# A six-layer decoder kernel on one core: the first two weights loaded and split in tiles, the start's loads reordered, the first extra rows issued by two engines

## The chip, the cores and the metric

The kernel runs on one core of a Trainium2 chip. The metric is the device time of one execution in microseconds (us). Engines are named as in the profile: PE (TensorE; PEld is its weight load), DVE (VectorE), ACT (ScalarE), POOL (GpSimd), SP (SyncE, which only issues transfers here); SPq is SP's sequencer.

## The reference, cut to what matters

Two decoder layers over `x` (8 batches, 128 tokens, 512 features, float32). Layer 0: causal attention of 32 heads, autocorrelation against a context, a mixture of 28 low-rank experts. Layer 1: attention with ALiBi slopes, cross attention, routed low-rank heads. A layer norm follows each. The change lies in the first microseconds of layer 0's attention:

```
q = (x @ Wq.T + bq).reshape(b, l, h, hd).transpose(0, 2, 1, 3)
k = (x @ Wk.T + bk).reshape(b, l, h, hd).transpose(0, 2, 1, 3)
v = (x @ Wv.T + bv).reshape(b, l, h, hd).transpose(0, 2, 1, 3)
scores = jnp.einsum('bhqd,bhkd->bhqk', q, k) / math.sqrt(hd)
att = softmax(where(causal, scores, -inf)); out = att @ v;  out @ Wo.T + bo
```

## The kernel before, in words

All of x stays on chip in `x_all`. A float32 product of weights is done in three matmuls (`mm3`, lines 736 to 738) of 128x512, on a high part and a low part of each operand: ACT writes the high part (a cast), DVE the low part (the difference). One product of a batch with a 512x512 weight is four tiles k of three matmuls, 12 in all.

Layer 0's attention is a software pipeline over steps i from -8 on, four steps a batch; each engine runs its own `attention_step(l, i)` in that order, and semaphores tie them. In the start the order of work on PE is: x of batch 0 turned (L791), q of batch 0 (12 matmuls), k of batch 0 (12), x of batch 1 turned, qT of batch 0 turned (L814), kT of batch 0 turned, q and k of batch 1, then step 0: `scores` of step 0 (L855), x of batch 2 turned, qT of batch 1; step 1: `scores` of step 1, v of batch 0, kT of batch 1; step 2: `scores` of step 2, q of batch 2; and so on. Step i's `scores` wait for the row maxima of step i-1, two reductions on DVE (`maxima`, L2045). Three banks of PSUM are shared in turn (`bank_taken`): a product may start when the one two before it has been read.

Weights of layer 0's attention come whole, 1 MB each, by SP. `first_weights(i)` splits one: on ACT two casts of 128x1024 (L1326), on DVE two differences of 128x1024 (L1989). Weights q and k are split before the pipeline starts; v in step -3, o in step 0. On ACT the split of v lies between the two `qk_split` (L1337) of batch 0: that of qT and that of kT. `tables` on DVE (L1993, L1994) makes bf16 copies of the identity and of the mask; it stands before the steps and waits for seven small loads counted on one semaphore, `ld_c`, the last of which is `br_row`. After it come the `biased` additions (L2018) that free q's and k's banks.

The rows of masks and positions that `scores` need beside q and k come by small transfers (`extra_rows`, L661): eight of 16 KB a batch, issued by SP once both of the batch's `qk_split` are done.

SP's order at the start is: x of batch 0, the identity (L632), weight q (L633), bq and bk (L635), small (L636), weight k (L637), the mask (L638), x of batch 1, weight v (L640), bv, bo, br (L641 to L643), weight o (L644), x of batches 2 to 7, two contexts (L622), two pieces of a later weight (L619), and then the extra rows of batch 0.

Of the kernel before, what the change touches and what calls it, by code (L numbers as in the profile page):

```python
# [109 lines left out]
def decoder(nc, a, out):  # L110
# [9 lines left out]
    with es:  # L120
# [178 lines left out]
        ld_w0 = [sem(f"ld_w0_{n}") for n in "qkvo"]  # L299
        ld_masks = sem("ld_masks")  # L300
# [9 lines left out]
        x_loaded = per_slot("x_loaded")  # L310
        x_rest = sem("x_rest")
# [57 lines left out]
        mix_psum = per_slot("mix_psum")  # L369
        mixmax_ready = per_slot("mixmax_ready")  # L370
        mixexp_ready = per_slot("mixexp_ready")
        mixed_ready = per_slot("mixed_ready")
        mixedT_psum = per_slot("mixedT_psum")
        mixedT_ready = per_slot("mixedT_ready")
# [30 lines left out]
        TABLES, EARLY = 2, 7  # L405
# [107 lines left out]
        START = FIRST + 6  # L513

# [19 lines left out]
        def mix(trip, y):  # L534

            return nth(trip, 1, 1, TRIPS if y == FF else 0)
# [71 lines left out]
        def _(sp):  # L608
# [3 lines left out]
            def load_x(b):  # L612
                sp.dma_start(x_all[:, b, :], row(a["x"], b)).then_inc(x_loaded[b] if b < SLOTS else x_rest, 16)
# [41 lines left out]
            def extra_rows(l, b):  # L655

                sp.wait_ge(qk_rows, batch(l, b, 2, 2))
                for e in range(2):
                    for g in range(GROUPS):
                        at = g * PAD + HD * (1 - e) + 1  # L660
                        sp.dma_start(qk[b % RING][at:at + 4, e:e + 3:2, :, :], a["extra"][l, e, g]).then_inc(extra_loaded[b % 2], 16)  # L661

            def self_attention(l):

                pieces, before = ((pieces_during_A0, 0), (pieces_during_A1, PIECES_A1))[l]
                fetch(pieces(0), 0, 2, before, slice(0, 2))
                for i in range(FIRST, LAST):
# [12 lines left out]
                    if of_step(i, "kT") is not None:  # L680
                        extra_rows(l, b + 1)

            for s in both:
                load_context(a["ctx"], s, s)
# [46 lines left out]
        def _(pe):  # L731
# [46 lines left out]
            def x_rows_turned(l, b):  # L778
# [5 lines left out]
                elif b < SLOTS:  # L784
                    pe.wait_ge(x_loaded[b], 16)
                else:
                    pe.wait_ge(x_rest, 16 * (B - SLOTS))
# [6 lines left out]
            def projected(l, kind, b):  # L794
# [85 lines left out]
            def attention_out(l, b):  # L880
# [4 lines left out]
                if l == 0 and b == 0:  # L885
                    pe.wait_ge(w0_ready, 8)
# [126 lines left out]
            def gates_and_rank(trip, s):  # L1013
# [3 lines left out]
                ins.then_inc(mix_psum[s], 1)  # L1017
# [6 lines left out]
            def gated_to_rank(trip, s):  # L1024
                pe.wait_ge(mixed_ready[s], mix(trip, MOE))
# [3 lines left out]
                ins.then_inc(mixedT_psum[s], 1)  # L1029

            def experts_out(trip, s):
                pe.wait_ge(mixedT_ready[s], mix(trip, MOE))
# [101 lines left out]
            def routes_and_low(trip, s):  # L1134
# [5 lines left out]
                ins.then_inc(mix_psum[s], 1)  # L1140

            def low_to_rank(trip, s):
                pe.wait_ge(mixed_ready[s], mix(trip, FF))
                nc.tensor.transpose(bank[s][2][:, 0:P], low[s], ident[:, :]).then_inc(mixedT_psum[s], 1)
# [11 lines left out]
            pe.wait_ge(ld_masks, 16)  # L1156
# [133 lines left out]
        def _(act):  # L1290
# [30 lines left out]

            def first_weights(i):

                act.wait_ge(ld_w0[i], 16)
# [3 lines left out]
            def qk_split(l, i, b):  # L1328
# [5 lines left out]
                if l == 0 and b == RING - 1 and i == 0:  # L1334
                    act.wait_ge(w0_ready, 6)
# [3 lines left out]
                ins.then_inc(qk_rows, 1)  # L1339

# [8 lines left out]
            def probs(l, j):  # L1349
# [3 lines left out]
                if l == 0 and j < STEPS:  # L1353
                    act.wait_ge(w0_ready, 4)
# [12 lines left out]
            def attention_step(l, i):  # L1367
# [15 lines left out]
                if l == 0 and i in (-3, 0):  # L1383
                    first_weights(2 + (i == 0))
# [80 lines left out]
            def gate_exp(trip, s):  # L1465
                act.wait_ge(mixmax_ready[s], mix(trip, MOE))
                av(gates[s][:, 2, 0:NE], gates[s][:, 0, 0:NE], ACT.Exp, bias=st[s][:, ONE_A], scale=1.0
                   ).then_inc(mixexp_ready[s], 1)

            def gated_split(trip, s):  # L1470
                act.wait_ge(mixedT_psum[s], mix(trip, MOE))
# [74 lines left out]
            def route_exp(trip, s):  # L1546
                act.wait_ge(mixmax_ready[s], mix(trip, FF))
                av(st[s][:, EIGHT], st[s][:, EIGHT], ACT.Exp, bias=st[s][:, ONE_A], scale=1.0,
                   accum_out=st[s][:, ONE_B]).then_inc(mixexp_ready[s], 1)

            def low_copied(trip, s):
                act.wait_ge(mixedT_psum[s], mix(trip, FF))
# [12 lines left out]
            for i in range(2):  # L1565
                first_weights(i)
# [917 lines left out]
```

## Time and profile before

| | us |
|---|---|
| median of 3 runs (lowest to highest) | 955.42 (952.87 to 955.94) |
| the profiled execution | 953.89 |
| its span | 952.1 |
| PE busy in the span | 873.2 (92%) |
| first weight matmul of q | 12.44 |
| first `scores` matmul | 34.53 |

Times in the rows are us from the span's start. The span is what the profiler's rows cover; the execution's time holds 1.8 us around it. A timeline row gives start, duration, engine, line, operation and tiles, and, in brackets, how long the engine had been idle and who released it. A chain row gives start, length and what stood on the chain that ended last. A windows row gives the busy time of each engine in a stretch, then PE's granted clock (1.00 is full), the share of time that the DMA engines were busy, and GB/s.

### The profile page before, as it was taken

To read this page: it belongs to the slowest core of one execution; us is meant where nothing else is said; L and a number is where in the kernel's file an instruction comes from. 1 tells how busy PE (TensorE), PEld (TensorE's weight loads), DVE (VectorE), ACT (ScalarE), POOL (GpSimd) and SP (SyncE) were. 2 spreads that over 40 slices of the span, in tenths; PEclk is the share of its full clock that TensorE was granted. 3 is DMA by queue.
4 is the path that set the end of the run, shared out by engine and by line. 5 is a ranking of instruction groups with operands and counts; after the bars stand their busy time and mean duration, and the time that the engine had idled before them with its cause. 6 is when DMAs were issued, how large, how long until landed. Compare 5 with 4: busy or idle time off the path is not lost.

```text
span 952.1 us, 21348 instructions
## 1 busy us (share of the span) xinstructions
PE 873.2 (92%) x8680; PEld 697.4 (73%) x8680; DVE 584.5 (61%) x1506; ACT 395.5 (42%) x976; POOL 340.9 (36%) x356
## 2 busy tenths in 40 slices
PE   4899999797798989889999898999999999999995
PEld 3677777564444767667777677888998898889983
DVE  3445565657796556546666553797376747765765
ACT  3334444343555233224343333553454364526532
POOL 1111223267877346544777355770000000010001
PEclk9799999998999999889999899999999999999997
DMA  8100000122232110000000011231000010000001
GB/s 315 43 19 26 19 14 19 42 80 78 85 96 60 67 44 19 5 19 19 18 18 24 17 28 55 87 103 36 23 2 1 1 45 1 2 1 23 2 2 44
DMA packets 20945, 38.09 MB, mean 40 GB/s; under 512 B 3232, under 2 KB 7456, under 8 KB 20336
## 3 DMA queue, kind: packets, MB, share of 16 engines
q1 hardware_dynamic: 20848, 36.73, 12.4%
q8 instruction: 69, 1.13, 0.5%
q14 instruction: 28, 0.23, 0.1%
HBM read 30.20 MB, written 2.10 MB: 34 GB/s over the span
## 4 chain that ended last, share of the span: by engine, by line
PE 71%; DVE 11%; POOL 6%; issue 4%; DMA 3%; ACT 2%; SPq 2%; POOLq 0%; DVEq 0%; ACTq 0%
PE bank L736 15%; PE bank L737 14%; PE bank L738 14%; PE bank L855 7%; PE bank L1119 6%; PE bank L876 3%; DVE tank L2255 2%; PE bank L829 2%; PE bank L814 2%; DVE tank L2265 2%; PE bank L860 1%; DMA br_row<-br_dram 1%; PE bank L755 1%; DVE tank L2045 1%; PE bank L1150 1%
## 5 line engine op out<-in xcount | busy, mean ns | idle before, releaser
L736 PE MATMUL bank<-wr,hTl 128*128 128x512 f32 (+3 forms) x472 | 191.9, 407 | 10.8 <-DVE wr L1989 7.6
L737 PE MATMUL bank<-wr,hTh 128*128 128x512 f32 (+3 forms) x472 | 182.4, 386 | 0.0
L738 PE MATMUL bank<-wr,hTh 128*128 128x512 f32 (+3 forms) x472 | 182.2, 386 | 0.0
L2045 DVE TENSOR_REDUCE tank<-bank 128x4 f32<-128x512 f32 x128 | 82.4, 686 | 70.7 <-PE bank L829 70.7
L736 PEld LDWEIGHTS bank<-wr,hTl 128*128 128x128 f32 (+1 forms) x472 | 91.2, 193 | 35.6 <-issue 16.9
L1358 ACT ACTIVATE pT<-bank 128x512 f32<-128x512 f32 x128 | 69.5, 595 | 96.9 <-PE bank L829 96.8
L738 PEld LDWEIGHTS bank<-wr,hTh 128*128 128x128 f32 (+1 forms) x472 | 90.5, 192 | 17.8
L737 PEld LDWEIGHTS bank<-wr,hTh 128*128 128x128 f32 (+1 forms) x472 | 91.1, 193 | 15.4 <-issue 1.2
L855 PE MATMUL bank<-qk 32*128 32x128 f32 x1024 | 79.7, 297 | 15.3 <-DVE tank L2045 5.8
L855 PEld LDWEIGHTS bank<-qk 32*128 32x128 f32 x1024 | 66.9, 198 | 31.6 <-issue 24.6
L1337 ACT ACTIVATE qk<-bank,small_sb 128x512 f32<-128x512 f32 x64 | 46.3, 774 | 75.6 <-PE bank L814 75.6
L860 PE MATMUL bank<-qk 32*128 32x128 f32 x1024 | 77.0, 290 | 0.3 <-DMA qk<-tank 0.3
L736 PE MATMUL bank<-hTh,wr 128*128 128x256 f32 (+1 forms) x240 | 73.3, 305 | 1.5 <-DVE hTl L2226 1.5
L737 PE MATMUL bank<-hTl,wr 128*128 128x256 f32 (+1 forms) x240 | 73.0, 304 | 0.0
L738 PE MATMUL bank<-hTh,wr 128*128 128x256 f32 (+1 forms) x240 | 72.9, 304 | 0.0
L1775 POOL TENSOR_TENSOR stats<-stats,half 128x1 f32<-128x1 f32 x8 | 4.4, 548 | 180.2 <-DVE stats L2300 180.2
L1536 ACT ACTIVATE tank<-bank,stats 128x256 f32<-128x256 f32 x128 | 58.6, 482 | 21.7 <-DVE stats L2249 21.7
L860 PEld LDWEIGHTS bank<-qk 32*128 32x128 f32 x1024 | 64.5, 192 | 4.0 <-issue 3.0
L1119 PE MATMUL bank<-tank 128*32 128x128 f32 (+1 forms) x1024 | 53.8, 284 | 2.8 <-DVE tank L2255 1.8
L1764 POOL TENSOR_TENSOR stats<-stats,half 128x1 f32<-128x1 f32 x16 | 9.9, 621 | 127.0 <-DVE stats L2134 126.8
L2248 DVE TENSOR_REDUCE stats<-bank 128x2 f32<-128x512 f32 x64 | 43.7, 684 | 17.6 <-PE bank L738 17.6
L2255 DVE COPY tank<-bank 128x512 f32<-128x512 f32 x64 | 39.7, 682 | 21.8 <-PE bank L1108 21.8
(234 smaller groups left out, 1898.4 us busy)
## 6 DMA issues: line engine op xcount, KB each, us to landing
raw<-w_qkv_dram SPq DMA_DIRECT2D x12, 256.0 KB, 3.1
raw<-w_xq_dram SPq DMA_DIRECT2D x16, 192.0 KB, 2.3
raw<-w_xo_dram SPq DMA_DIRECT2D x12, 256.0 KB, 2.7
x_all<-x_dram SPq DMA_DIRECT2D x8, 256.0 KB, 11.5
cin<-ctx_dram SPq DMA_DIRECT2D x8, 256.0 KB, 3.2
qk<-extra_dram SPq DMA_DIRECT2D x128, 16.0 KB
cin<-ctxT_dram SPq DMA_DIRECT2D x8, 256.0 KB, 2.9
out_dram<-x_all SPq DMA_DIRECT2D x8, 256.0 KB, 2.0
```

The source lines that it names most:

```text
L736: mm(dst, lhs[1], rhs[0], start=start, stop=False)
L737: mm(dst, lhs[0], rhs[1], start=False, stop=False)
L738: return mm(dst, lhs[0], rhs[0], start=False, stop=stop)
L855: ins = mm(s_bank[n][:, at], qk[b % RING][g, e, m, :], qk[b % RING][g, 2 + e, m, :], start=m == 0, stop=True, skip_group_check=True)
L860: ins = mm(t_bank[n][:, at], qk[c % RING][g, 2 + f, m, :], qk[c % RING][g, f, m, :], start=m == 0, stop=True, skip_group_check=True)
L1119: ins = mm(bank[s][0][row:row + n, tile * P:(tile + 1) * P], xv[s][:, t * NKV + g * XD + first:t * NKV + g * XD + first + n], xpT[s][:, (2 ...
L1337: ins = av(qk[b % RING][:, 2 * i + e, :, :], tiles(m_bank[u % 2][:, :]), ACT.Identity, bias=row_shift[:, 2 * i + e:2 * i + e + 1], scale=r ...
L1358: av(pT[e][:, 2 * rows + n, :], t_bank[n][:, :], ACT.Exp).then_inc(exp_ready, 1)
L1536: ins = av(xp[s][:, h * XT:(h + 1) * XT], bank[s][i][:, j * XT:(j + 1) * XT], ACT.Exp, bias=st[s][:, NEGMAX.start + h:NEGMAX.start + h + 1 ...
L2045: v.tensor_reduce(nm[b % 2][:, at:at + KT], s_bank[n][:, :].rearrange("p (m t) -> p m t", m=KT), AX, ALU.max, negate=True).then_inc(max_re ...
L2248: steps_done(XA, trip, v.tensor_reduce(r, bank[s][i][:, :].rearrange("p (h t) -> p h t", h=2), AX, ALU.max))
L2255: v.tensor_copy(xpT[s][:, i * 512:(i + 1) * 512], bank[s][i][:, :]).then_inc(xpT_ready[s], 1)
```

## The change

The loads of weights q and k are cut in four tiles of 128x512 each, with a semaphore each, and so are their splits; PE waits tile by tile. The order of SP's loads is changed: bq follows q's tiles and bk follows k's; x of batch 2 comes right behind bv; weight o, x of batches 3 to 7, the contexts and the pieces of the later weight are issued after the extra rows of batch 0. The small loads that `tables` waits for are four now (bq, bk, small, mask); bv, bo and br are counted on another semaphore, for which DVE's `values` of batch 0 and POOL's first `add_bias` wait. Weights v and o are split in steps -1 and 4, on DVE after that step's `biased`. Of the eight extra rows of batch 0 ACT issues four. To free semaphores, six pairs (one semaphore per slot) are merged to one each, with counts that go over both slots.

```diff
-        ld_w0 = [sem(f"ld_w0_{n}") for n in "qkvo"]
-        ld_masks = sem("ld_masks")
+        ld_w0_tiles = [[sem(f"ld_w0_{n}{k}") for k in range(KT)] for n in "qk"]
+        ld_w0 = [sem(f"ld_w0_{n}") for n in "vo"]
-        mix_psum = per_slot("mix_psum")
+        mix_psum = sem("mix_psum")
...
-        TABLES, EARLY = 2, 7
+        TABLES, EARLY, ROWS = 2, 4, 3
+        W0_TILES = 2 * KT
+        W0_STEPS = (-1, 4)
...
-        def mix(trip, y):
-            return nth(trip, 1, 1, TRIPS if y == FF else 0)
+        def mix(trip, s, y):
+            return row_of(trip + (TRIPS if y == FF else 0), s)
...
             load_x(0)
-            sp.dma_start(ident[:, :], a["masks"][:, 0:P]).then_inc(ld_masks, 16)
-            sp.dma_start(raw_w0(0), a["w0_q"]).then_inc(ld_w0[0], 16)
-            for i, n in enumerate(("bq", "bk")):
-                sp.dma_start(by_column[i], a[n].partition_broadcast(P)).then_inc(ld_c, 16)
+            sp.dma_start(ident[:, :], a["masks"][:, 0:P]).then_inc(x_loaded[0], 16)
+            for i, n in enumerate("qk"):
+                for k in range(KT):
+                    at = slice(k * D, (k + 1) * D)
+                    sp.dma_start(raw_w0(i)[:, at], a["w0_" + n][:, at]).then_inc(ld_w0_tiles[i][k], 16)
+                sp.dma_start(by_column[i], a["b" + n].partition_broadcast(P)).then_inc(ld_c, 16)
             sp.dma_start(small[:, :], a["small"]).then_inc(ld_c, 16)
-            sp.dma_start(raw_w0(1), a["w0_k"]).then_inc(ld_w0[1], 16)
             sp.dma_start(causal, a["masks"][:, P:]).then_inc(ld_c, 16)
             load_x(1)
-            sp.dma_start(raw_w0(2), a["w0_v"]).then_inc(ld_w0[2], 16)
-            sp.dma_start(bv_row, a["bv"].partition_broadcast(P)).then_inc(ld_c, 16)
-            sp.dma_start(bo_row, a["bo"].partition_broadcast(P)).then_inc(ld_c, 16)
-            sp.dma_start(br_row[:, :], a["br"].partition_broadcast(P)).then_inc(ld_c, 16)
-            sp.dma_start(raw_w0(3), a["w0_o"]).then_inc(ld_w0[3], 16)
-            for b in range(SLOTS, B):
-                load_x(b)
+            sp.dma_start(raw_w0(2), a["w0_v"]).then_inc(ld_w0[0], 16)
+            sp.dma_start(bv_row, a["bv"].partition_broadcast(P)).then_inc(ld_rows, 16)
+            load_x(2)
+            sp.dma_start(bo_row, a["bo"].partition_broadcast(P)).then_inc(ld_rows, 16)
+            sp.dma_start(br_row[:, :], a["br"].partition_broadcast(P)).then_inc(ld_rows, 16)
...
                 for e in range(2):
-                    for g in range(GROUPS):
-                        at = g * PAD + HD * (1 - e) + 1
-                        sp.dma_start(qk[b % RING][at:at + 4, e:e + 3:2, :, :], a["extra"][l, e, g]).then_inc(extra_loaded[b % 2], 16)
+                    if (l, b, e) != (0, 0, 0):
+                        for g in range(GROUPS):
+                            at = g * PAD + HD * (1 - e) + 1
+                            sp.dma_start(qk[b % RING][at:at + 4, e:e + 3:2, :, :], a["extra"][l, e, g]).then_inc(extra_loaded[b % 2], 16)
...
                     if of_step(i, "kT") is not None:
                         extra_rows(l, b + 1)
+                    if l == 0 and of_step(i, "kT") == 0:
+                        fetch(pieces(0), 0, 2, before, slice(0, 2))
+                        sp.dma_start(raw_w0(3), a["w0_o"]).then_inc(ld_w0[1], 16)
+                        for n in range(RING, B):
+                            load_x(n)
+                        for s in both:
+                            load_context(a["ctx"], s, s)
...
 PE, projected:
-                if l == 0 and b == 0:
-                    pe.wait_ge(w0_ready, 2 * (i + 1))
                 for k in range(KT):
+                    if l == 0 and b == 0:
+                        pe.wait_ge(w0_ready, KT * i + k + 1 if kind in "qk" else W0_TILES + 2)
...
 ACT:
+            def first_tiles(i):
+                for k in range(KT):
+                    act.wait_ge(ld_w0_tiles[i][k], 16)
+                    copy(w_qkv0[i][0][:, k], tiles(raw_w0(i))[:, k]).then_inc(w0_hi, 1)
+            def extra_rows_of_first():
+                act.wait_ge(qk_rows, 2)
+                for g in range(GROUPS):
+                    at = g * PAD + HD + 1
+                    act.dma_start(qk[0][at:at + 4, 0:3:2, :, :], a["extra"][0, 0, g]).then_inc(extra_loaded[0], 16)
                 if of_step(i - 1, "kT") is not None:
                     qk_split(l, 1, b + 1)
+                    if l == 0 and b + 1 == 0:
+                        extra_rows_of_first()
...
-                if l == 0 and i in (-3, 0):
-                    first_weights(2 + (i == 0))
+                if l == 0 and i in W0_STEPS:
+                    first_weights(2 + W0_STEPS.index(i))
...
 POOL, ahead of the steps:
-            pool.wait_ge(ld_c, 16 * EARLY)
+            pool.wait_ge(ld_rows, 16 * ROWS)
 DVE (values of batch 0 waits for ld_rows too):
+            def first_tiles(i):
+                for k in range(KT):
+                    dve.wait_ge(w0_hi, KT * i + k + 1)
+                    v.tensor_tensor(w_qkv0[i][1][:, k], tiles(raw_w0(i))[:, k], f32(w_qkv0[i][0][:, k]), ALU.subtract).then_inc(w0_ready, 1)
-                if l == 0 and i in (-3, 0):
-                    first_weights(2 + (i == 0))
                 for n, kind in enumerate("qk"):
                     if of_step(i, kind) is not None:
                         (biased, clipped)[l](n, b + 2)
+                if l == 0 and i in W0_STEPS:
+                    first_weights(2 + W0_STEPS.index(i))
             for i in range(2):
-                first_weights(i)
-            dve.wait_ge(ld_masks, 16)
+                first_tiles(i)
+            dve.wait_ge(x_loaded[0], 32)
             dve.wait_ge(ld_c, 16 * EARLY)
             tables()
```

## Rows read from the trace of the kernel before

**Rows 1.** The page, busy time of the engines

```profile
PE 873.2 (92%) x8680; PEld 697.4 (73%) x8680; DVE 584.5 (61%) x1506; ACT 395.5 (42%) x976; POOL 340.9 (36%) x356
```

**Rows 2.** The chain of waits, 0 to 80 us: start, length, what

```profile
8.40 10.69 DMA br_row<-br_dram
19.19 1.36 DVE ident L1993
...
30.50 4.03 issue
34.53 1.96 PE bank L855 x16
...
46.28 1.09 PE bank L855 x16
...
62.66 0.31 PE bank L855 x2
```

**Rows 3.** Timeline, 0 to 21 us: start, duration, engine, line, operation

```profile
4.88 0.58 ACT L1320 CAST hTh<-bank 128x512 fp32r<-128x512 f32 x1 [2.88 <-PE bank L791]
5.50 0.69 DVE L1983 TENSOR_TENSOR hTl<-bank,hTh 128x512 fp32r<-128x512 f32 x1 [5.50 <-ACT hTh L1320]
8.86 1.99 ACT L1326 CAST wr<-pT 128x1024 fp32r<-128x1024 f32 x2 [3.40 <-DMA pT<-w_q_dram]
9.94 2.36 DVE L1989 TENSOR_TENSOR wr<-pT,wr 128x1024 fp32r<-128x1024 f32 x2 [3.75 <-ACT wr L1326]
12.44 0.77 PE L736 MATMUL bank<-wr,hTl 128*128 128x512 f32 x1 [7.60 <-DVE wr L1989]
17.68 0.40 PE L736 MATMUL bank<-wr,hTl 128*128 128x512 f32 x1
20.25 0.40 PE L738 MATMUL bank<-wr,hTh 128*128 128x512 f32 x1
20.57 1.27 DVE L2018 TENSOR_TENSOR tank<-bank,tank 128x512 f32<-128x512 f32 x2
```

**Rows 4.** Timeline, 21 to 26 us

```profile
21.99 0.63 PE L814 MATMUL bank<-ident,tank 128*128 128x128 f32 x4
22.66 1.45 ACT L1337 ACTIVATE qk<-bank,small_sb 128x512 f32<-128x512 f32 x2
23.52 0.63 PE L814 MATMUL bank<-ident,tank 128*128 128x128 f32 x4 [0.90 <-DVE hTl L1983]
24.00 2.00 ACT L1326 CAST wr<-qk 128x1024 fp32r<-128x1024 f32 x2
```

**Rows 5.** Transfers, 0 to 60 us: KB, issue to landing; line L661, 26 to 36, then 0 to 60

```profile
pT<-w_k_dram SPq DMA_DIRECT2D x1, 1024.0 KB, 9.8
...
L661 SPq DMA_DIRECT2D qk<-extra_dram x8: 613/628/834, 27.4 to 32.2; - x8
...
L661 SPq DMA_DIRECT2D qk<-extra_dram x16: 613/627/834, 27.4 to 52.4; - x16
```

**Rows 6.** The loads of x (line L613), 0 to 60 us: issue to landing

```profile
DMA to landing us min/median/max: 2.8/11.5/12.0
```

**Rows 7.** Windows of 1 or 2 us

```profile
5.00:6.00 1.00, 0.00 (x0) 0.00 (x0) 0.50 (x1) 0.47 (x1) 0.00 (x0) 1.00 0.76 262
6.00:7.00 1.00, 0.00 (x0) 0.00 (x0) 0.19 (x1) 0.00 (x0) 0.00 (x0) 1.00 0.97 389
22.00:23.00 1.00, 0.62 (x5) 0.38 (x4) 0.32 (x1) 0.93 (x2) 0.89 (x1) 1.00 1.07 406
35.00:36.00 1.00, 1.00 (x12) 1.00 (x12) 0.00 (x0) 0.00 (x0) 0.00 (x0) 0.50 0.00 0
```

**Rows 8.** Timeline, 44 to 60 us

```profile
44.98 0.40 PE L736 MATMUL bank<-wr,hTl 128*128 128x512 f32 x1
57.41 1.45 ACT L1337 ACTIVATE qk<-bank,small_sb 128x512 f32<-128x512 f32 x2
59.17 1.29 DVE L2045 TENSOR_REDUCE tank<-bank 128x4 f32<-128x512 f32 x2 [0.93 <-PE bank L829]
```

More of the change, by code:

```diff
@@ L310, in decoder @@
         x_loaded = per_slot("x_loaded")
+        x_third = sem("x_third")
         x_rest = sem("x_rest")
@@ L368, in decoder @@
         mixture_ready = sem("mixture_ready")
-        mix_psum = per_slot("mix_psum")
[L370 to L374, printed above, removed]
+        mix_psum = sem("mix_psum")
+        mixmax_ready = sem("mixmax_ready")
+        mixexp_ready = sem("mixexp_ready")
+        mixed_ready = sem("mixed_ready")
+        mixedT_psum = sem("mixedT_psum")
+        mixedT_ready = sem("mixedT_ready")
         inner_hi = per_slot("inner_hi")
@@ L612, in load_x @@
             def load_x(b):
-                sp.dma_start(x_all[:, b, :], row(a["x"], b)).then_inc(x_loaded[b] if b < SLOTS else x_rest, 16)
+                sp.dma_start(x_all[:, b, :], row(a["x"], b)).then_inc((*x_loaded, x_third)[b] if b < RING else x_rest, 16)
             def fetch(pieces, trip, per_trip, before, which):
@@ L658, in extra_rows @@
                 for e in range(2):
-                    for g in range(GROUPS):
-                        at = g * PAD + HD * (1 - e) + 1
-                        sp.dma_start(qk[b % RING][at:at + 4, e:e + 3:2, :, :], a["extra"][l, e, g]).then_inc(extra_loaded[b % 2], 16)
+                    if (l, b, e) != (0, 0, 0):
+                        for g in range(GROUPS):
+                            at = g * PAD + HD * (1 - e) + 1
+                            sp.dma_start(qk[b % RING][at:at + 4, e:e + 3:2, :, :], a["extra"][l, e, g]).then_inc(extra_loaded[b % 2], 16)
             def self_attention(l):
                 pieces, before = ((pieces_during_A0, 0), (pieces_during_A1, PIECES_A1))[l]
-                fetch(pieces(0), 0, 2, before, slice(0, 2))
+                if l == 1:
+                    fetch(pieces(0), 0, 2, before, slice(0, 2))
                 for i in range(FIRST, LAST):
@@ L681, in self_attention @@
                         extra_rows(l, b + 1)
-            for s in both:
-                load_context(a["ctx"], s, s)
+                    if l == 0 and of_step(i, "kT") == 0:
+                        fetch(pieces(0), 0, 2, before, slice(0, 2))
+                        sp.dma_start(raw_w0(3), a["w0_o"]).then_inc(ld_w0[1], 16)
[3 more added lines that the diff above has]
+                            load_context(a["ctx"], s, s)
             self_attention(0)
@@ L784, in x_rows_turned @@
                 elif b < SLOTS:
-                    pe.wait_ge(x_loaded[b], 16)
+                    pe.wait_ge(x_loaded[b], 32 if b == 0 else 16)
+                elif b < RING:
+                    pe.wait_ge(x_third, 16)
                 else:
-                    pe.wait_ge(x_rest, 16 * (B - SLOTS))
+                    pe.wait_ge(x_rest, 16 * (B - RING))
                 u = m_uses[l, "x", b]
@@ L1139, in routes_and_low @@
                     ins = mm(bank[s][2][:, 0:NL], plain_hT[:, k, s, 1, :], w_al[:, k, :], start=k == 0, stop=k == KT - 1)
-                ins.then_inc(mix_psum[s], 1)
+                ins.then_inc(mix_psum, 1)
             def low_to_rank(trip, s):
-                pe.wait_ge(mixed_ready[s], mix(trip, FF))
-                nc.tensor.transpose(bank[s][2][:, 0:P], low[s], ident[:, :]).then_inc(mixedT_psum[s], 1)
+                pe.wait_ge(mixed_ready, mix(trip, s, FF))
+                nc.tensor.transpose(bank[s][2][:, 0:P], low[s], ident[:, :]).then_inc(mixedT_psum, 1)
             def heads_out(trip, s):
@@ L1353, in probs @@
                 if l == 0 and j < STEPS:
-                    act.wait_ge(w0_ready, 4)
+                    act.wait_ge(w0_ready, W0_TILES)
                 if b > 0 or l == 1:
@@ L2000, in values @@
                 dve.wait_ge(consts_ready, ONES[l])
+                if l == 0 and b == 0:
+                    dve.wait_ge(ld_rows, 16 * ROWS)
                 if b >= 2:
```

51 lines of the change are left out of this document (25 added, 26 removed).

## The prediction

> **What bounds the kernel now.** The page comes first: PE is busy 92% of the span [rows 1], so what can go is a stretch in which PE waits or runs slowly. The windows of the start show one, 0 to 46 us. Second, the chain of waits over that stretch: it runs through SP's issues to `br_row`'s landing at 19.1, DVE's `tables`, then PE, and has a hole of 4.03 us ahead of the first `scores` [rows 2]. Third, the timelines, which show what PE lacked in each gap: the split of q [rows 3], the two `qk_split` with the split of v between them [rows 4]. Last, the transfers [rows 5, 6]. From `scores` of step 2 (46.28) PE is nearly always busy up to 100 us, and everything behind is tied to the pipeline's steps, not to the clock on the wall; so I take the time at which `scores` of step 2 start as the measure, and look for what is given back behind it.
>
> **The parts.** All times are those of the profiled execution.
>
> 1. Tiles of q. Weight q landed at 8.86 and its first product began at 12.44, behind two casts and two differences [rows 3]. In the change the same bytes precede the last tile, so it lands at 8.86 again; the bytes behind tile 0 are three tiles, 0.79 MB, which at 262 to 389 GB/s [rows 7] take 2.0 to 3.0 us. I take 2.5: tile 0 lands at 6.3, the others some 0.85 apart. A tile's split costs 0.6 on ACT (0.58 for a cast of 128x512) and 0.69 on DVE, with 0.1 between [rows 3]: ready at 7.7. Floor: DVE is busy with x until 6.19, so 6.9. Ceiling: the tiles land together at 8.86, ready at 10.2. A tile feeds 3 matmuls at half clock, 1.3 us (12 took 12.44 to 17.68 [rows 3]), slower than tiles arrive, so PE doesn't wait again. q runs 7.7 to 12.95, k at the full pitch (17.68 to 20.65, 2.97 us) 12.95 to 15.9. Weight k landed at 13.6 (3.78 + 9.8 [rows 5]); its last tile, now ahead of bk and small, is no later, is ready by 15.0, and its 0.7 us of matmuls fit. k ends 4.75 us earlier.
>
> 2. `tables` no longer wait for `br_row`. The first `biased` ended at 21.2, the second at 21.84, and qT began at 21.99, 1.34 behind k's end. Now `biased` of q can be done during k: qT begins 0.85 behind k's end, at 16.75, 5.2 us earlier. The L1993 copy took 1.36 us for 128 columns [rows 2]. If it takes that again right behind the last split, `biased` of q ends at 17.2 and qT is 1.2 us later. I take none of it, since in the change POOL's first addition waits for bv, bo and br.
>
> 3. Split of v. From qT's start to the end of kT's `qk_split`, at which the first extra row is issued, there are 5.35 us (21.99 to 27.36) [rows 4, 5], of which ACT's two casts of v hold 1.9 [rows 4]. Without them kT's rows are ready at 20.2, 7.1 us earlier. The cover is kT's turning, which ends 2.2 us behind qT's start.
>
> 4. Extra rows. Eight issues, 0.63 us each and 0.69 apart, with the landing made 7.17 us (27.36 to 34.53) [rows 2, 5]. Four on each engine save four pitches, 2.8 us: landed at 24.6. At the same time q and k of batch 1 (12 matmuls each, k free to start when kT's rows are ready) end at 24.7. So both ends meet, and `scores` of step 0 begin at 24.75, 9.8 us earlier. Lower bound of the saving here: the transfers of the two engines go one behind the other, as eight in one queue do, and nothing of the 2.8 comes. On ACT the issues stand ahead of the split of v, which then runs 23.0 to 25.0.
>
> 5. A new wait. DVE's half of v's split now stands behind `biased` of k (24.7 to 25.4) and takes 2.36 us: 25.4 to 27.75. The maxima of step 0 queue behind it, 27.75 to 29.05. PE has `scores` of step 0 (1.4 at full clock, chain row 46.28 with its mask), x and qT turned until 27.4, then waits for those maxima, 1.7 us. Steps 1's `scores`, v (2.9) and kT (0.6) follow: `scores` of step 2 at 34.1.
>
> 6. Clock. Behind the hole of 4.03 us PE's granted clock was 0.50 [rows 7], the lower of its two levels, 1.2 GHz, and matmuls had the long pitch until 44.98 [rows 8]. `scores` of step 0 to those of step 2 took 11.75 us; mine take 9.35 with the new wait in. The saving at `scores` of step 2 is 46.28 - 34.1 = 12.2.
>
> 7. Split of o in step 4. ACT would do it behind the `qk_split` that ends at 58.86, DVE 3.35 us later has its lower part (24.00 to 27.35 for v [rows 4]), at 62.2. Maxima of step 5 began at 59.17 [rows 8] and would now end at 63.5, where PE wants them at 62.66 [rows 2]: 0.9 us lost. The bounds are 0 and 2.4, its whole time on DVE.
>
> 8. At nothing: the merged semaphores (each engine goes through slot 0, then slot 1, as before), the loads moved behind the extra rows (3.3 MB at 406 GB/s [rows 7], 8 us from 23 on, landed near 33; x of batch 3 is wanted at step 4, near 44, the piece that ACT splits in step 1 lands first), POOL's additions. The extra rows of batch 1 are the cover that could go. Their last issue stood at 52.4 [rows 5]; with the 2.3 us from last issue to first use in batch 0 (32.2 to 34.53) they landed near 54.7, and `scores` of step 4 began near 55 (two steps of 4.3 us behind 46.28): no slack. In the change they may be issued from 35.6 on. SP's ten moved issues, from 23 on at 0.5 to 0.9 us, end at 28 to 32, and their bytes have landed near 33, so I count nothing; if they took longer than to 35.6, each further us would be lost.
>
> Sum: 12.2 - 0.9 = 11.3 us. The profiled execution gives 953.89 - 11.3 = 942.6; the median of the runs is 1.5 above it, so I predict 944.1.
>
> Two rules of the Trainium skill bear on this. The first, in "DMA: Bandwidth & Descriptors", section Bandwidth, says to batch transfers to 1 MiB or more to get three quarters of the peak. Weight q's loads go against it, but loads of 256 KB with rows of 2 KB ran at 406 GB/s when queued behind each other [rows 7]; by that rule the last tile of k would be late, as in the rival on the other side. The second, same page, section Issuing engines are not separate DMA queues, says that issuing on several engines saves only the sequencer's own time, usually small. Here the eight issues are most of the hole, so by the trace the saving of part 4 stands and by the rule's word "small" it would shrink to the case of one behind the other.
>
> **The rivals.**
>
> Tiles don't come early. The 16 engines' shares of the tiles finish together, and PE starts at 10.2. For: the long landing times of queued loads (9.8 and 11.5 us) [rows 5, 6] show that many are in flight. Against: they land in order. Price 2.5: 946.6.
>
> The clock stays low. Between 24.75 and 29.1 PE does little; if the clock falls there, v and the `scores` run at the long pitch, as at 35 to 45 us. For: the fall behind a wait of 4 us. Against: from 20.65 to 24.2 PE was idle nearly half the time and kept its pitch. Price: v 2.2, `scores` 1.0, the rest 0.3: 3.5, so 947.6.
>
> The extra rows of two engines go one behind the other. Then they land at 27.4; the maxima end at 30.1 instead of 29.05, since v's split is already done, so the wait of part 5 takes most of it. Price 1.3 at most: 945.4. This is also the case in which the change doesn't do what it says.
>
> The other side, slower. Each tile costs what a lone load costs, 2.8 us issue to landing (the shortest of x's [rows 6]). Nine loads (eight tiles, bq) from 3.7 on end at 29; k's product ends at 31 instead of 20.65, 10.4 later, of which parts 2 to 7 give back 6.5: 959. It decides from 2.4 us a tile on (k's end at 27.2). A queued pace of 0.7 (256 KB at 389 to 406 GB/s [rows 7]) speaks against it. In a milder form, near 2.4, there is no change; so there is if a later stage gives the whole saving back, for which I see no transfer or engine tied to absolute time.
>
> **How the numbers follow.** My case 0.58; tiles late 0.12; clock 0.13; one behind the other 0.07; no change 0.06; slower 0.04. The time is my case's, 944.1. Its own bounds are the floor of part 1 (-0.8), part 7 at 0 (-0.9) and, above, `tables` (+1.2) and part 7 whole (+1.5), to which the spread of the runs before adds 2.5 below and 0.5 above. The range goes from 938.5, which also leaves room for the wait of part 5 not coming (-1.7), to 950, where the tiles' and the clock's prices meet. About 0.3% (2.9 us) is what a measurement of this kernel can tell from no change: faster by more 0.90, within 0.06, slower 0.04.
>
> **What would show it.** In the changed kernel's timeline: the first L736 matmul at 7.7 (right within 1); k's last matmul near 15.9; the first L855 near 24.75, against 34.53; a wait of 1 to 2 us of PE for L2045 ahead of the second group of L855; the third group near 34; no granted clock of 0.50 between 20 and 45 us; a wait of near 1 us for L2045 in step 6. The forecast fails if PE's first weight matmul comes after 10, or if the interval from `scores` of step 2 to the end, 905.8 us now (952.1 - 46.3), grows by more than 3 us.

## The result, and the profile after

The changed kernel takes 943.24 us (median of four runs; 940.63 to 944.06) where the kernel before, run beside it, takes 954.9: a ratio of 0.9882, 95% interval 0.9861 to 0.9904, 11.7 us less. Its profiled execution took 944.06, 9.8 less than the one before. The forecast was 944.1.

The page of the changed kernel, busy time of the engines, answers to [rows 1]. Neither PE's work nor its share has changed to speak of; the span has.

```profile
span 942.2 us, 21361 instructions
PE 870.5 (92%) x8680; PEld 695.7 (74%) x8680; DVE 582.5 (62%) x1510; ACT 396.8 (42%) x980; POOL 340.8 (36%) x356
```

The timeline of the changed kernel's start, the marks that the prediction named (start, duration, engine, line, operation; rows between them are left out; lines 745, 802, 825, 866, 2078 are 736, 791, 814, 855, 2045 of before):

```profile
5.61 0.62 ACT L1336 CAST wr<-pT 128x512 fp32r<-128x512 f32 x1 [0.20 <-DMA pT<-w_q_dram]
7.10 0.77 PE L745 MATMUL bank<-wr,hTl 128*128 128x512 f32 x1 [2.31 <-DVE wr L2014]
...
13.89 0.22 DVE L2024 CAST ident<-ident 128x128 bf16<-128x128 f32 x1
14.13 0.68 DVE L2051 TENSOR_TENSOR tank<-bank,tank 128x512 f32<-128x512 f32 x1
15.36 0.60 PE L802 MATMUL bank<-ident,x_all 128*128 128x128 f32 x4
16.39 0.63 PE L825 MATMUL bank<-ident,tank 128*128 128x128 f32 x4 [0.44 <-DVE tank L2051]
...
23.18 1.99 ACT L1342 CAST wr<-qk 128x1024 fp32r<-128x1024 f32 x2 [3.33 <-issue]
24.96 1.16 PE L866 MATMUL bank<-qk 32*128 32x128 f32 x16 [0.48 <-issue]
25.13 2.35 DVE L2020 TENSOR_TENSOR wr<-qk,wr 128x1024 fp32r<-128x1024 f32 x2
27.40 1.28 DVE L2078 TENSOR_REDUCE tank<-bank 128x4 f32<-128x512 f32 x2
28.73 1.16 PE L866 MATMUL bank<-qk 32*128 32x128 f32 x16 [1.36 <-DVE tank L2078]
30.15 0.80 PE L745 MATMUL bank<-wr,hTl 128*128 128x512 f32 x1
34.97 1.16 PE L866 MATMUL bank<-qk 32*128 32x128 f32 x16
```

To be seen: PE starts on the first tile, 5.3 us ahead of [rows 3]; the first `scores` come at 24.96 instead of 34.53, with 0.48 us of pause where 4.03 were [rows 2]; ahead of the second, at 28.73, stands the new wait of 1.36 us for the maxima, which had queued behind v's split; and the third, at 34.97, is 11.2 us ahead of the same matmul before (46.21 in that kernel's timeline; its chain, [rows 2], has the step's `scores` from 46.28).

Windows of the changed kernel between the second and third `scores`; PE's granted clock is the number behind POOL's. It fell to 0.50 (1.2 GHz, the lower level) for 3.4 us, where before it was 0.50 for 10.2 us from 34.7 on [rows 7, 8]:

```profile
29.00:30.00 1.00, 1.00 (x24) 0.83 (x22) 0.28 (x1) 0.19 (x1) 0.72 (x1) 0.92 0.96 391
30.00:31.00 1.00, 1.00 (x10) 0.75 (x3) 0.73 (x2) 0.00 (x0) 0.00 (x0) 0.50 1.05 399
31.00:32.00 1.00, 1.00 (x3) 0.74 (x3) 0.56 (x1) 0.00 (x0) 0.00 (x0) 0.50 1.05 391
32.00:33.00 1.00, 1.00 (x4) 0.78 (x3) 0.00 (x0) 0.00 (x0) 0.00 (x0) 0.50 1.04 399
33.00:34.00 1.00, 1.00 (x6) 0.79 (x5) 0.00 (x0) 0.00 (x0) 0.00 (x0) 0.88 1.03 385
```

And the timeline of step 4 to 6, where o is split now; it answers to [rows 8]:

```profile
47.50 2.00 ACT L1342 CAST wr<-tank 128x1024 fp32r<-128x1024 f32 x2
48.59 2.36 DVE L2020 TENSOR_TENSOR wr<-tank,wr 128x1024 fp32r<-128x1024 f32 x2 [1.59 <-ACT wr L1342]
50.86 1.28 DVE L2078 TENSOR_REDUCE tank<-bank 128x4 f32<-128x512 f32 x2
52.20 0.38 PE L866 MATMUL bank<-qk 32*128 32x128 f32 x2 [0.78 <-DVE tank L2078]
```

The lead of the changed kernel, matching matmul for matmul (both have 8680): 5.3 at the first product, 6.0 at the turning of x of batch 1, 9.6 at the first `scores`, 9.9 at the second, 11.2 at the third, 10.4 from step 6 on, 8.9 from 171 us on, 8.3 from 332, 8.5 from 640, 9.9 at the last. So in this pair of traces the start gives 10.4, and the code behind it, which is the same, moves it by 2.1 down and 1.5 up: a fall of the clock at 163 us lasts 6.8 us where before it lasted 3.4, and the last one begins 7.8 us ahead of the end where before it did 12.9. A second trace of each kernel (experiment 9) gives 8.5 at the third `scores`, 7.6 from step 6 on and 9.8 at the last: what the start gives is 7.6 to 10.4 us, by the execution.

### The profile page after: what moved, and what is told of

Its sections match the earlier page's. It is cut to its first block, busy times and chain, and to the rows that moved or that the text cites. A ratio compares the mean times of both kernels' runs of the same rounds, so it can differ in the third digit from the quotient of the medians.

```text
span 942.2 us, 21361 instructions
## 1 busy us (share of the span) xinstructions
PE 870.5 (92%) x8680; PEld 695.7 (74%) x8680; DVE 582.5 (62%) x1510; ACT 396.8 (42%) x980; POOL 340.8 (36%) x356
## 4 chain that ended last, share of the span: by engine, by line
PE 73%; DVE 10%; POOL 6%; issue 4%; DMA 3%; ACT 2%; SPq 2%; POOLq 0%; DVEq 0%; ACTq 0%
PE bank L745 16%; PE bank L746 15%; PE bank L747 15%; PE bank L866 6%; PE bank L1130 6%; PE bank L887 3%; DVE tank L2288 2%; PE bank L840 2%; PE bank L825 1%; PE bank L871 1%; DVE tank L2298 1%; DVE tank L2078 1%; PE bank L764 1%; SPq L664 1%; PE bank L1150 1%
## 5 line engine op out<-in xcount | busy, mean ns | idle before, releaser
L746 PEld LDWEIGHTS bank<-wr,hTh 128*128 128x128 f32 (+1 forms) x472 | 91.3, 194 | 15.4 <-issue 1.2
L1353 ACT ACTIVATE qk<-bank,small_sb 128x512 f32<-128x512 f32 x64 | 46.2, 775 | 76.4 <-PE bank L825 76.4
L1569 ACT CAST hTh<-bank 128x384 fp32r<-128x384 f32 x32 | 15.3, 480 | 91.0 <-PE bank L1130 91.0
```

Source lines behind the costliest of these rows:

```text
L746: mm(dst, lhs[0], rhs[1], start=False, stop=False)
L1353: ins = av(qk[b % RING][:, 2 * i + e, :, :], tiles(m_bank[u % 2][:, :]), ACT.Identity, bias=row_shift[:, 2 * i + e:2 * i + e + 1], scale=r ...
```

## The experiments

Each is one kernel, profiled once and timed beside the kernel before on one chip (955.3 beside experiments 1 to 4, 953.7 beside 5 to 8, 953.6 beside the second runs of experiment 8 and those of 9). Times of one kernel scatter by 5 to 10 us, so the medians carry the size of an effect and the marks of the start its cause. In experiments 1 to 3 the 95% intervals of the ratio overlap that of the changed kernel (0.9861 to 0.9904): their 2 us in the median are not clear of the scatter, and only the marks speak there. The marks scatter too: the second trace of the kernel before has them 1.4 to 2.0 us earlier, with weight q landed at 7.45 and not at 8.86. "First", "second" and "third" are the starts of the `scores` of steps 0, 1 and 2; lines shift by a few between the kernels.

| kernel | median us | first product | x of batch 1 turned | first | second | third |
|---|---|---|---|---|---|---|
| before | 954.9 | 12.4 | 21.4 | 34.5 | 38.7 | 46.2 |
| before, second trace | 952.9 | 11.0 | 20.0 | 33.2 | 36.7 | 44.8 |
| changed | 943.2 | 7.1 | 15.4 | 25.0 | 28.7 | 35.0 |
| changed, second trace | 943.1 | 6.9 | 15.2 | 24.8 | 28.6 | 36.4 |
| whole loads | 945.7 | 9.8 | 18.2 | 28.2 | 31.6 | 36.3 |
| extra rows by SP | 945.4 | 7.1 | 15.1 | 26.8 | 29.6 | 34.3 |
| v split early | 945.2 | 7.0 | 15.1 | 26.6 | 29.4 | 34.1 |
| `tables` behind br | 951.8 | 6.9 | 21.4 | 32.0 | 35.9 | 42.2 |
| loads in front | 947.6 | 7.1 | 15.6 | 29.4 | 33.6 | 41.8 |
| before, 4 extra rows by ACT | 948.0 | 11.8 | 21.4 | 32.4 | 35.2 | 41.0 |
| tiles alone | 953.6 | 7.4 | 21.9 | 35.7 | 40.0 | 47.1 |
| low parts on POOL | 939.5 | 7.5 | 15.1 | 24.5 | 27.3 | 32.0 |
| low parts on POOL, second trace | 940.6 | 7.6 | 15.3 | 25.0 | 27.8 | 32.5 |

**1. Whole loads.**

```diff
-                for k in range(KT):
-                    sp.dma_start(raw_w0(i)[:, at], a["w0_" + n][:, at]).then_inc(ld_w0_tiles[i][k], 16)
+                sp.dma_start(raw_w0(i), a["w0_" + n]).then_inc(ld_w0_tiles[i][0], 16)
...
-                    act.wait_ge(ld_w0_tiles[i][k], 16)
+                    act.wait_ge(ld_w0_tiles[i][0], 16)
```

> The changed kernel, with weights q and k loaded whole again (one transfer each, in the same place of SP's order); split and waited for in tiles as in the changed kernel. Theory (the tiles' early landing starts PE): all four tiles land when the whole did before, 8.9, the first product begins at 8.9 + 0.6 + 0.7 + 0.15 = 10.3 instead of 7.1, and the third group of `scores` comes near 38 instead of 35.0; near 946.3, 3 us over the changed kernel's 943.2. Rival 1 (loads of 256 KB cost bandwidth, so whole loads land earlier as a sum): PE starts later, but k's last tile lands well before 12, and the loss is under 1 us. Rival 2 (the gain of the start came from the split in tiles on ACT and DVE, not from the loads): the first product begins before 9.

945.67 (942.31 to 947.65), ratio to before 0.9897 (0.9858 to 0.9936). Its timeline where the weights arrive:

```profile
8.33 2.18 ACT L1334 CAST wr<-pT 128x512 fp32r<-128x512 f32 x4 [3.08 <-DMA pT<-w_q_dram]
9.82 0.76 PE L743 MATMUL bank<-wr,hTl 128*128 128x512 f32 x1 [5.18 <-DVE wr L2012]
12.29 2.18 ACT L1334 CAST wr<-pT 128x512 fp32r<-128x512 f32 x4 [1.78 <-DMA pT<-w_k_dram]
```

The first product came at 9.8, and the 2.7 us ran through to the second `scores` (+2.9); the third is only 1.4 later than in the changed kernel's trace, since no fall of the clock came in this one. The early landing of tile 0 (5.61 against 8.33) is these 2.7 us of the start, so rival 2 is out. But the split in tiles has a share of its own: from landing to first product it takes 1.49 us here and in the changed kernel, 3.58 in the kernel before (8.86 to 12.44 [rows 3]). Of the 5.3 us by which PE starts earlier, 2.1 come from the split. Rival 1 is out too: weight k, whole, was there at 12.29, hardly before the last tile's cast of the changed kernel (12.6), and the first two `scores` kept the whole delay.

**2. Extra rows by SP.**

```diff
-                    if (l, b, e) != (0, 0, 0):
-                        for g in range(GROUPS):
+                    for g in range(GROUPS):
...
-                    if l == 0 and b + 1 == 0:
-                        extra_rows_of_first()
```

> The changed kernel, with all eight extra rows of batch 0 issued by SP again. Theory (the issuing sequencer is the price, 0.63 to 0.69 us each): the first `scores` begin 7.2 us after the first issue, near 27.0 instead of 24.97, since eight issues end 2.8 us later; the maxima of step 0 then no longer wait for v's split, so the second group of `scores` comes near 30.0 instead of 28.7, and the pause of PE from 24.5 to 27 may lengthen the fall of the clock from 3.4 to 6.8 us or more. 945 to 947, against 943.2. Rival (two engines' transfers go one behind the other anyway): the first `scores` stay at 25.0 and the time at 943.2.

945.41 (942.15 to 949.92), 0.9896 (0.9866 to 0.9927). Its timeline:

```profile
24.90 2.35 DVE L2017 TENSOR_TENSOR wr<-qk,wr 128x1024 fp32r<-128x1024 f32 x2
26.80 1.16 PE L865 MATMUL bank<-qk 32*128 32x128 f32 x16 [2.54 <-issue]
28.23 1.29 DVE L2075 TENSOR_REDUCE tank<-bank 128x4 f32<-128x512 f32 x2 [0.98 <-PE bank L839]
29.58 1.16 PE L865 MATMUL bank<-qk 32*128 32x128 f32 x16 [0.37 <-DVE tank L2075]
```

The first `scores` are 1.8 us later, the second 0.9: half of the delay is cover for v's split. At the first `scores` the issues are the price, as the theory has it. Over the whole, nothing is lost in this trace: its third `scores` come 0.7 earlier than the changed kernel's, which had a fall of the clock there, and it took 942.15. The longer fall of the clock that I had thought possible is not there: behind a pause of 2.54 us there was none at all.

**3. v split early.**

```diff
-        W0_STEPS = (-1, 4)
+        W0_STEPS = (-3, 4)
```

> The changed kernel, with v split in step -3 again, between the two `qk_split` of batch 0 on ACT (o stays in step 4). Theory: kT's rows come 1.9 us later, so the extra rows are issued near 21.8 and the first `scores` begin near 26.9 instead of 24.97; but DVE is then free for the maxima, PE no longer waits 1.36 us for them, and the second group comes near 29.7 instead of 28.7: 1 us lost, 944.2 (with the fall of the clock unchanged). Rival (the wait for the maxima is what lets the clock fall): no granted clock of 0.50 between 25 and 40 us, and 942 to 943. Second rival (the moved split is worth its whole 1.9 us): 945.1.

945.23 (942.34 to 950.85), 0.9908 (0.9882 to 0.9935). First 26.6, second 29.4, as the theory said. No granted clock of 0.50 between 25 and 40 us, which is the first rival's sign; its time isn't there, for the median is 2 us over the changed kernel's, though this is within the scatter, and the profiled execution (942.34) would have fitted.

**4. `tables` behind br.**

```diff
             dve.wait_ge(ld_c, 16 * EARLY)
+            dve.wait_ge(ld_rows, 16 * ROWS)
             tables()
```

> The changed kernel, with `tables` on DVE waiting for bv, bo and br as before. Theory (the tiles' gain hangs on this edit: `biased` of q queues behind `tables`, and br lands at 18.95): `tables` start near 19.0 and end near 20.4 (POOL adds at the same time), x of batch 1 is turned from 21.1 on instead of 15.4, the first `scores` come near 30.5, and the time is near 949, 5 to 6 us over the changed kernel's. Rival (as the prediction sized this edit, 0.5 us): 943.7.

951.76 (947.86 to 954.01), 0.9973 (0.9949 to 0.9997). Its timeline between k's end and the next matmul:

```profile
19.18 1.26 POOL L1733 TENSOR_TENSOR x_all<-x_all,tank 128x512 f32<-128x512 f32 x1 [17.02 <-DMA br_row<-br_dram]
19.23 1.29 DVE L2024 CAST ident<-ident 128x128 bf16<-128x128 f32 x1 [5.24 <-DMA br_row<-br_dram]
20.44 0.18 DVE L2025 CAST causal<-tank 128x64 bf16<-128x64 f32 x1
20.55 1.27 DVE L2051 TENSOR_TENSOR tank<-bank,tank 128x512 f32<-128x512 f32 x2
21.37 1.09 PE L802 MATMUL bank<-ident,x_all 128*128 128x128 f32 x4 [6.25 <-DVE tank L2051]
```

One wait on three small loads, the last of 4 KB, costs 6.0 us at this mark, and 8.5 in the median: behind PE's pause of 6.25 us the clock fell at 20.1 for 6.8 us as well, which the expectation of 949 had left out. In the kernel before, the same wait cost almost nothing, because k ended at the same time as `tables`.

**5. The kernel before with four of the extra rows by ACT.**

```diff
+                    if (l, b, e) != (0, 0, 0):
...
...
+                    if l == 0 and b + 1 == 0:
+                        extra_rows_of_first()
```

> The kernel before with one edit: ACT issues four of the eight extra rows of batch 0. Theory (each of the change's effects is there by itself, and the pause of 4.03 us is what let the clock fall for 10.2 us): the first `scores` begin 2.8 us earlier, near 31.8; PE's pause shrinks to 1.3 us, the clock keeps its upper level, and `scores` of step 2 come near 39.5 instead of 46.3: near 948. Rival 1 (the clock falls there whatever the pause, since the stretch of small matmuls behind it is weak work): 2.8 us gained only, 952. Rival 2 (no gain without the tiles): 954.9.

948.02 (946.74 to 952.05), 0.9947 (0.9928 to 0.9966) of 953.73. Its timeline:

```profile
32.43 1.16 PE L856 MATMUL bank<-qk 32*128 32x128 f32 x16 [1.90 <-issue]
35.21 1.16 PE L856 MATMUL bank<-qk 32*128 32x128 f32 x16 [0.38 <-DVE tank L2055]
37.33 2.36 DVE L1999 TENSOR_TENSOR wr<-tank,wr 128x1024 fp32r<-128x1024 f32 x2 [1.58 <-ACT wr L1327]
39.61 1.28 DVE L2055 TENSOR_REDUCE tank<-bank 128x4 f32<-128x512 f32 x2
40.95 1.16 PE L856 MATMUL bank<-qk 32*128 32x128 f32 x16 [0.93 <-DVE tank L2055]
```

A pause of 1.90 us instead of 4.03, and no fall of the clock: the first `scores` are 2.1 us earlier, the third 5.3 (0.8 and 3.9 against the second trace of the kernel before, whose start was early throughout, with the same pause of 4.02). This one edit brings half of the change's gain. It also uncovers a wait: o's split in step 0, hidden before by v's product at the long pitch, now delays the maxima, and PE waits 0.93 us for them (with the first `scores` 0.6 us later than expected, the 1.5 by which the third mark missed 39.5).

**6. Tiles alone.** Weights q and k in tiles (loads, splits, waits), everything else as before. The diff is against the changed kernel; SP's order of loads, DVE's order in steps -3 and 0 and the issuer of the extra rows are set back too.

```diff
-        W0_STEPS = (-1, 4)
+        W0_STEPS = (-3, 0)
...
             dve.wait_ge(ld_c, 16 * EARLY)
+            dve.wait_ge(ld_rows, 16 * ROWS)
             tables()
```

> Tiles alone: weights q and k are loaded and split in tiles and waited for by tile, while the order of all loads, `tables` behind br, the steps of v's and o's splits, DVE's order and the eight extra rows by SP are those of the kernel before. Theory (the tiles' 5.3 us are taken back at once by `tables`, which wait for br at 19.1): the first product begins near 7.1, k ends near 16, and from the turning of x of batch 1 on (21.4) everything is where it was: 953 to 955, no gain. Rival (the tiles carry the gain): 949.

953.61 (948.09 to 957.62), 0.9995 (0.9971 to 1.002). The waits of this kernel from 10 to 25 us (engine, line, what it waited for: us in total, times, longest):

```profile
PEld bank L801 <- issue: 5.4, 1, 5.4
PE bank L801 <- DVE tank L2048: 5.0, 1, 5.0
DVE ident L2021 <- DMA br_row<-br_dram: 3.9, 1, 3.9
```

All 5 us of the early start wait for br. The clock fell at 21.4, behind this pause, for 6.8 us, and at 35.0 for 10.2, with a pause of 3.18 us ahead of the first `scores`. The part that gives the change its name gains nothing alone.

**7. Loads in front.**

```diff
+                if l == 0:
+                    sp.dma_start(raw_w0(3), a["w0_o"]).then_inc(ld_w0[1], 16)
+                    for n in range(RING, B):
+                        load_x(n)
+                    for s in both:
+                        load_context(a["ctx"], s, s)
+                fetch(pieces(0), 0, 2, before, slice(0, 2))
...
```

> The changed kernel, with weight o, x of batches 3 to 7, the two contexts and the two pieces of a later weight issued ahead of the extra rows of batch 0, as before. Theory (the extra rows queue behind 3.3 MB): the bulk lands near 27.5, so the extra rows, issued at 19.9, land behind it near 28.5 or later, instead of 24.9; the second group of `scores` comes near 31.5, the clock falls for longer, and the time is 946 to 949. Rival (small transfers pass the bulk, or SP's issue order doesn't matter): first `scores` at 25, 943.2.

947.64 (945.44 to 950.5), 0.9942 (0.9923 to 0.9961). The same eight extra rows, issued at the same time by the same two engines:

```profile
19.83 2.87 SPq L664 DMA_DIRECT2D qk<-extra_dram x4
19.84 3.24 ACTq L1360 DMA_DIRECT2D qk<-extra_dram x4
...
29.38 2.08 PE L864 MATMUL bank<-qk 32*128 32x128 f32 x16 [5.14 <-issue]
```

All eight were there only at 29.4, 4.4 us later, and with the pause of 5.14 us came a fall of 13.7 us. ACT's own queue helps little past SP's bulk: the packets of its four transfers moved between 24.1 and 27.4, where in the changed kernel they moved between 21.4 and 24.4, so they ended 3.0 us later; SP's own four, behind the bulk in the same queue, came last. The third `scores` are 6.8 later and the median 4.4. From there to the last matmul this trace took 894.5 us where the changed kernel's took 899.9, and had the clock low for 44 us in all where that had it low for 58; so the one doesn't measure the other to the microsecond.

**8. Low parts on POOL.** POOL computes the low part of v's second half in step -1 and of o in step 4; DVE keeps v's first half and waits for o's before its tank is written again.

```diff
-                for e in range(2):
+                for e in range(1 if i == 2 else 0):
...
+                if l == 0 and i == W0_STEPS[0]:
+                    pool.wait_ge(w0_hi, W0_TILES + 2)
+                    nc.gpsimd.tensor_tensor(half_w0(2, 1, 1), raw_half(2, 1), f32(half_w0(2, 0, 1)), ALU.subtract).then_inc(w0_ready, 1)
...
```

> The changed kernel, with the low part of v's second half and both halves of o's low part computed on POOL instead of DVE. Theory (DVE's queue is what makes PE wait ahead of the second `scores`, 1.36 us, and in step 6, 0.8 us): the maxima of step 0 begin near 26.4, the second group of `scores` near 27.8 instead of 28.7, the wait in step 6 is gone, and with a shorter pause the clock may stay up (another 1.7 us): 939.8 to 941.5. Rival (POOL's difference of 128x1024 takes over 3 us, or slows DVE beside it, and v's product waits for it instead): the second group is earlier but v's first matmul is at 30 or later, as now, and only step 6's 0.8 us are gained: 942.4.

> The kernel with the low parts of v's second half and of o on POOL once more, on one chip with the changed kernel. Theory (PE's two waits for DVE are gone, 1.4 and 0.8 us, as its first trace showed, and at times 1.7 us of low clock): 2 to 4 us under the changed kernel in the same call, near 939. Rival (its 939.5 was the scatter between chips and executions): within 1 us of the changed kernel.

939.52 (936.26 to 943.69), 0.9861 (0.9829 to 0.9894), and a second time, on one chip with the changed kernel, 940.64 (936.79 to 946.99), 0.9859 (0.9823 to 0.9894). The first trace:

```profile
24.64 1.22 DVE L2027 TENSOR_TENSOR wr<-qk,wr 128x1024 fp32r<-128x1024 f32 x1
24.74 3.32 POOL L1783 TENSOR_TENSOR wr<-qk,wr 128x1024 fp32r<-128x1024 f32 x1 [3.10 <-ACT wr L1342]
25.93 1.29 DVE L2085 TENSOR_REDUCE tank<-bank 128x4 f32<-128x512 f32 x2
27.28 1.16 PE L866 MATMUL bank<-qk 32*128 32x128 f32 x16 [0.37 <-DVE tank L2085]
28.59 0.50 PE L745 MATMUL bank<-wr,hTl 128*128 128x512 f32 x1
```

Both waits for DVE are gone (0.37 us remain of 1.36, and step 6 follows the third `scores` by 16.4 us instead of 17.2), and neither trace had the clock fall before 160 us. POOL's difference did take over 3 us, as the rival has it, but it was done at 28.06, ahead of v's first matmul. The medians are 3.7 and 2.5 us below those of the changed kernel; the ranges overlap, and so do the intervals of the ratio on the one chip (0.9823 to 0.9894 against 0.9842 to 0.9904). All twelve times, with a median of 939.8, stand against ten with 943.1. At step 6 the two traces lead the changed kernel's two by 3.8 and 4.7 us, of which 1.5 and 3.1 are that kernel's fall of the clock; 2.3 and 1.7 are left for the two waits and the start's scatter.

**9. The changed kernel and the kernel before once more.**

> The changed kernel once more, unedited, for a second trace of its start and more times on one chip with the two others of this call. Theory (the fall of the clock at 30 us in its first trace came by chance of time, since two variants with pauses of 2 to 2.5 us before their `scores` had none): the same marks, first product near 7.1, first `scores` near 25.0, second near 28.7, and either a fall of 3.4 us again or none; with none, `scores` of step 2 near 33.3 instead of 35.0. 941 to 944. Rival (the 1.36 us wait for the maxima brings the fall each time): 0.50 between 29 and 34 us again, `scores` of step 2 at 35.0.

> The kernel before once more, for a second trace of its start. Theory (a pause of 4.03 us lets the clock fall in every execution, while how long it stays low varies): a granted clock of 0.50 from about 34 on for 6.8 or 10.2 us, `scores` of step 0 at 34.5 and of step 2 near 46.3 or 44.5; 954. Rival (this fall too comes by chance): no 0.50 before 100 us, `scores` of step 2 near 42.

943.09 (939.01 to 945.24), ratio 0.9873 (0.9842 to 0.9904); and 952.87 (948.21 to 955.19) for the kernel before. The changed kernel's second trace has the clock fall again, earlier and for 6.8 us; windows of 4 us (PE's granted clock again behind POOL's number):

```profile
24.00:28.00 4.00, 2.71 (x34) 1.97 (x32) 3.65 (x5) 2.20 (x5) 1.18 (x1) 1.00 0.86 215
28.00:32.00 4.00, 3.44 (x27) 2.83 (x28) 2.15 (x4) 1.00 (x3) 1.14 (x2) 0.58 0.99 382
32.00:36.00 4.00, 4.00 (x13) 3.09 (x12) 0.24 (x1) 0.00 (x0) 0.00 (x0) 0.56 0.61 228
```

Its third `scores` came at 36.4. The second trace of the kernel before has a fall of 10.2 us too, at 34.0, behind a pause of 4.02; its first product came at 11.0 instead of 12.4, so the lead at that mark is 3.9 to 5.6 us, by the pair of executions that one takes. The fall in both traces of the changed kernel and none in experiments 1, 2, 3, 5 and 8 fit the rival of the expectation better than mine, and experiment 4 fits it too: a wait of 1.55 us for the maxima, and a fall of 3.4 us at 37.1. But experiments 2 and 3 had longer pauses, ahead of the first `scores`, without a fall, and no run took away that wait and nothing else; so the wait goes with the fall in three traces of three and is not shown to be its cause.

## Why the prediction was right, step by step

The time (944.1 against 943.24) and the sign were right, by the mechanism of my case, with part of a rival in it. That the two lie within 0.9 us is luck in part: the profiled execution was forecast at 942.6 and took 944.06, 1.5 too slow, and the median, put 1.5 above the profiled execution, came 0.8 below it; the two errors cancelled.

Part 1, right and a little small. Tile 0 landed at 5.6, not 6.3, as its split began then; PE started at 7.10 (forecast 7.7) and k ended at 15.4 (15.9). The forecast 4.7 us at this mark were 2.6 of landing and 2.2 of the finer split; measured were 3.3 and 2.1. The ceiling of 10.2 was near what whole loads give (9.8, experiment 1).

Part 2, right at the mark (qT at 16.39, forecast 16.75), but mis-weighed. I sized the edit by what it changes beside the other edits, half a microsecond. Taken away alone it costs 6.0 us at the turning of x and 8.5 in all (experiment 4), and without it part 1 is worth nothing (experiment 6). The L1993 copy took 0.22 us, so the bound of 1.36 did not come.

Part 3, right: kT's rows were ready at 19.87 (forecast 20.2). Alone it is worth 1.6 at the first `scores` and 0.6 at the second (experiment 3), since it brings part 5's wait with it.

Part 4, right: the first `scores` at 24.96 (24.75), and the lower bound of transfers one behind the other is refuted for a free queue by experiment 2. It holds where there is bulk ahead (experiment 7).

Part 5, right: a wait of 1.36 us (1.7), the second `scores` at 28.73 (29.1).

Part 6 failed in its step on the clock, though not in the time of the whole. The sum had the clock up from 24.75 on; in both traces of the changed kernel it fell, for 3.4 and 6.8 us. In the first the third `scores` came 34.97 - 28.73 = 6.2 us behind the second, where the traces without a fall have 4.7: 1.5 us (3.1 in the second trace), against the 3.5 that the rival priced. The second mark had come 0.4 earlier than forecast and the stretch without a fall is 0.3 shorter (4.73 against 5.0), which leaves the 0.9 between the forecast 34.1 and 34.97. Why the clock fell there stays open (experiment 9).

Part 7, right: 0.78 us of wait (0.9), and experiment 8 takes it away.

Part 8: nothing late showed. The extra rows of batch 1 were issued from 36.55 on, behind SP's last moved issue at 28.8, and PE had no wait ahead of `scores` of step 4. Experiment 7 shows what moving the loads buys: 4.4 us.

The sum of 11.3 is 9.8 in both pairs of traces and 11.7 in the medians (10.5 in the second timing of the changed kernel, 943.09 beside 953.63). What the trace lacks is 0.9 at the third mark and 0.6 from the later stages (the interval from there to the end, 905.8 before, is 907.2), within the 3 us that I had allowed. The range's lower end is 0.3 above what its own terms give (944.1 - 0.8 - 0.9 - 1.7 - 2.5 = 938.2), which changes nothing here.

Of the rivals: tiles landing together is out (experiment 1 against the trace); the one on the other side, a lone load's cost for each tile, too: the casts of q's four tiles ran from 5.61 to 9.04, at most 1.4 us apart. The rule of the Trainium skill ("DMA: Bandwidth & Descriptors", Bandwidth) on large transfers is about the rate, and the rate may well have dropped a little: from 4 to 12 us the DMA engines moved 300 GB/s with the cut loads and 334 with the whole ones, in one trace each. That did not make k's last tile late enough to matter, and the first tile started PE 2.7 us earlier. What the same page says under Issuing engines are not separate DMA queues agrees in one half, that transfers of all issuers run on the same DMA engines (experiment 7), and the sequencer's time, which it calls usually small beside the DMA itself, was 1.8 us at the first `scores` (experiment 2).

## What to carry to other kernels

At a kernel's start several short chains end nearly together, and the gain of one edit shows only when the next chain is cut too: tiles alone gave nothing, and with them in place one wait on a 4 KB load was worth 8.5 us. Price an edit by taking it out of the finished version as well as by putting it in alone. A pause of the matmul engine is worth more than its length when the clock falls behind it: 2.1 us less pause brought 5.7 us in experiment 5. And where an elementwise job queues ahead of the reduction that the next matmuls wait for, an idle engine can take a part of it.

## What the runs showed of the hardware

POOL and DVE hinder each other. DVE's copy of 128x128 to bf16 took 0.22 us alone and 1.29 (1.36 before) beside a POOL addition of 1.26 that had begun 0.05 us earlier; POOL's difference of 128x1024 took 3.32 us when DVE's of the same kind had begun 0.1 earlier and ran 1.22, and 2.4 each later, with no difference of DVE's beside it (two in 4.74). That fits what the Trainium skill, "SBUF — State Buffer", SBUF: two separate sides, says of the port pair that the two share: whoever starts first holds it for the whole instruction. The delayed copy ended 0.08 us behind POOL's addition, at 20.52 and 20.44; POOL's difference ended 2.2 us behind DVE's.

The clock's falls in the start are not given by the length of the pause alone. Pauses of 3.2 to 6.3 us after q's product came with one each, six in five traces (6.8 to 13.7 us long); pauses of 1.9 to 2.5 us in three traces with none; and a pause of 1.4 to 1.6 us between the first and the second `scores`, with small matmuls on both sides, with one in three of three (one of 1.0 us there, in experiment 1, with none). What tells them apart stays open.

Ahead of the first fall the granted clock is no full guide. It reads 1.00 from the start in both kernels, yet q's twelve matmuls stood 0.43 us apart and k's 0.23 to 0.25, in the kernel before [rows 3] as in the changed one (7.10 to 12.40, then 12.40 to 15.4). The pitch shows what the column doesn't.

One trace is one execution: in times of one kernel on one chip the spread was 5 to 10 us, some of it from falls of the clock in stages that no edit touched.
